# Local attention: scores in quarters of the array, the queries' scale inside the exponentials, a new order of work

## The chip, the cores and the metric

The kernel runs on one core of one Trainium2 chip. The core has TensorE (PE, with PEld for the loading of its stationary operand), VectorE (DVE), ScalarE (ACT), GpSimd (POOL) and SyncE (SP), which only issues transfers here. The metric is the device time of one execution in microseconds (us), lower is better.

## The reference

The input is 16 sequences of 256 tokens with 128 features, so 32 tiles of 128 tokens. The program is: cross attention, a local transformer of depth 2, cross attention again, a mixture of experts. The change is in the attention of the local transformer alone, which is run twice, once for each layer:

```python
h = shift_token(x)
q, k, v = split(h @ wqkv)               # 8 heads of 64
q = q / max(norm(q), 1e-12) * q_scale
k = k / max(norm(k), 1e-12) * k_scale
q, k = rotary_xpos(q, k)                # q * cos + swap_halves(q) * sin, the same for k
# windows of 64 tokens; a query sees its own window and the one before
sim = where(mask, -max, 8 * q @ k.T)    # 64 queries x 128 keys for each head and window
o = softmax(sim) @ v
x = x + o @ wo
```

## The kernel before, in words

Every engine has its own program, written out by hand, and semaphores connect them. The phases stand one behind the other, and all engines meet at the end of each. The phases of local attention (class `Local`, tiles with the prefix `a_`) are the second and the fourth. In such a phase a loop over `s` runs on each engine; in turn `s` the engine does one piece of work for several tiles at once, each at another stage: "`s - 5`" means the tile that came in five turns ago. The order of the pieces within a turn is the order in which the engine does them, and it is this order that the change rewrites. One turn is one tile of 128 tokens.

The stages of one tile, with the lines of the profile:

- L677 to L680, SP: the tile comes into `h`, half of its features shifted by a token. L779, PE: `h` is transposed into `ps_a`. L852, ACT, and L935, DVE, make `hT` and its rounding rest `hTr`.
- L740 to L742, PE: queries and keys into `ps_qk` (two halves of 512 columns, three matmuls each), and with the same lines the values into `ps_b`.
- L872 and L884, ACT: squares of queries and of keys. L921, DVE: their sums for 16 heads (8 of queries, 8 of keys). L997 and L999, POOL: the maximum with 1e-24 and the power -1/2.
- L972 and L975, DVE: products with the table of cosines and, in two pieces of 256 columns with halves swapped, of sines; they go to `rot` and `rot2`. L946, DVE, adds the two for the queries, L995, POOL, for the keys. L1003, POOL, multiplies queries and keys, 1024 columns, by the 16 powers.
- L813, PE: eight transposes of `rot`. L954, DVE: two copies of 64 partitions put the queries into `qbd`, whose other half stays zero, so that the two heads of a pair lie block by block. L878, ACT: the keys into `kTr`.
- L756, PE: the mask is written into the two banks of `ps_s` as a bfloat16 matmul with the identity. L769: eight fp32 matmuls of 128 x 128 add the scores, each for a pair of heads and one window. An fp32 matmul with its weight load has two records each in the trace.
- L928, DVE: maxima over the 128 keys of eight rows. L865, ACT: eight exponentials of 128 x 128 with the maximum as bias, and each followed by the record that reads the accumulated sum. L959, DVE: reciprocals. L1009, POOL: the exponentials, 1024 columns, times the reciprocals.
- L787, PE: eight transposes of the exponentials. L858, ACT: the copy to `eT`, 1024 columns. L803, PE: sixteen matmuls of 64 columns with the values, into two halves of the partitions. L941, DVE: the copy to `oT`. L832, PE: four matmuls with `lwo`. L981, DVE: the sum with the layer's input.
- L891 and L900, ACT: for one window of two tiles the values have to stand in other partitions; half tiles are copied to `vx`. L894 copies the values to `vt`.

The order on ACT in a turn is: L852 (`s - 1`), L858 (`s - 6`), the eight L865 (`s - 5`), L872 (`s - 2`), L878 (`s - 4`), L884 (`s - 2`), L894 (`s - 4`). So tile t's `eT` stands directly ahead of tile t + 1's exponentials. The order on POOL is: L995, L997, L999 and L1003 of tile `s - 3`, then L1009 of tile `s - 5`.

## Time and profile before

| what | us |
|---|---|
| median of 3 runs (1401.6 to 1405.2) | 1403.48 |
| the profiled execution: its own time | 1405.5 |
| its span, first to last instruction | 1403.1 |
| first phase of local attention (from L845 at 228.4 to the last L981 at 539.9), second (629.0 to 945.5) | 311.5, 316.5 |
| busy over the span: PE, DVE, ACT, POOL | 1211.3, 1120.5, 874.9, 877.2 |

The busy times are those of the whole span; the two phases of local attention make up 628 us of it. "Clock" is the TensorE clock that was granted, 1.00 being 2.4 GHz. In the timeline a line stands for one instruction or for several alike in a row ("x8"), with start, length from the first start to the last end, engine and line; a bracket tells for how long the engine had been idle and who released it. Two instructions in a row overlap by a little, so what one costs is the distance between two starts rather than its length.

### The profile page before, as it was taken

Reading aid. Unit: us, or ns where it says so; the run is one execution under the profiler, and the core shown is the slowest. Engines: PE = TensorE matmul, PEld = TensorE weight load, DVE = VectorE, ACT = ScalarE, POOL = GpSimd, SP = SyncE. Lnnn points to the kernel's source line nnn. Section 1 sums busy time; section 2 is a strip of 40 time slices with the busy share of each in tenths; the row PEclk is TensorE's granted clock in tenths of the full one; section 3 lists DMA queues with packets and bytes.
Section 4 is the critical chain, followed back from the end, with each engine's and each line's share of the span. In section 5 each row is a group of like instructions: output and inputs, shape, how many; then the busy total and the mean of one; then the engine's idle time right before and its main releaser. Section 6 shows DMA issues by size and latency. Waiting matters only on the chain.

```text
span 1403.1 us, 32333 instructions
## 1 busy us (share of the span) xinstructions
PE 1211.3 (86%) x10768; PEld 1050.1 (75%) x10768; DVE 1120.5 (80%) x2622; ACT 874.9 (62%) x2445; POOL 877.2 (63%) x1070
## 2 busy tenths in 40 slices
PE   5588774799999994984999999977979999899997
PEld 3466553688888884983788888867966777699997
DVE  3799995899999972775899999946878998488887
ACT  1376662577777772553777777744547777466664
POOL 0567763999999971325999999933346664233342
PEclk9699996999999997996999999998979999899999
DMA  6100000000000001111000000001110000000000
GB/s 166 50 1 2 1 1 15 8 9 9 10 9 9 4 1 47 32 29 23 9 9 9 9 9 8 2 2 30 30 48 2 2 2 1 2 15 13 13 12 14
DMA packets 59411, 23.36 MB, mean 17 GB/s; under 512 B 49093, under 2 KB 57074, under 8 KB 59250
## 3 DMA queue, kind: packets, MB, share of 16 engines
q1 hardware_dynamic: 55296, 19.22, 5.8%
q10 hardware_dynamic: 3954, 2.09, 0.6%
q8 instruction: 90, 1.47, 0.4%
q14 instruction: 71, 0.58, 0.1%
HBM read 10.81 MB, written 2.10 MB: 9 GB/s over the span
## 4 chain that ended last, share of the span: by engine, by line
PE 58%; DVE 18%; issue 9%; ACT 7%; POOL 3%; SPq 2%; DMA 2%; ACTq 1%; DVEq 0%; POOLq 0%
PE a_ps_s L769 7%; PE m_ps_h L1191 7%; PE m_ps_y L1201 6%; DVE x_e L622 5%; DVE x_stat L619 5%; PE a_ps_b L803 4%; PE a_ps_t L813 4%; PE a_ps_t L787 4%; PE f_ps_y L1064 3%; PE a_ps_a L832 3%; PE f_ps_g L1073 3%; PE f_ps_a L1078 3%; ACT a_e L865 3%; ACT x_qhh L531 2%; PE a_ps_s L756 2%
## 5 line engine op out<-in xcount | busy, mean ns | idle before, releaser
L999 POOL TENSOR_TENSOR a_stat<-a_stat,small 128x16 f32<-128x16 f32 x64 | 186.9, 2921 | 5.3
L865 ACT ACTIVATE a_e<-a_ps_s,a_stat 128x128 f32<-128x128 f32 x512 | 179.6, 378 | 4.0 <-DVE a_stat L928 3.1
L769 PEld LDWEIGHTS a_ps_s<-a_kTr,a_qbd 128*128 128x128 f32 x1024 | 137.6, 195 | 4.3
L769 PE MATMUL a_ps_s<-a_kTr,a_qbd 128*128 128x128 f32 x1024 | 137.6, 278 | 0.0
L1009 POOL TENSOR_TENSOR a_e<-a_e,a_stat 128x1024 f32<-128x1024 f32 x64 | 121.4, 1897 | 23.7 <-DVE a_stat L959 23.7
L1003 POOL TENSOR_TENSOR a_rot<-a_rot,a_stat 128x1024 f32<-128x1024 f32 x64 | 121.8, 1903 | 5.0
L865 ACT ACTIVATION_READ_ACCUMULATOR a_e<-a_ps_s,a_stat 128x1 f32 x512 | 111.7, 218 | 0.0
L972 DVE TENSOR_TENSOR a_rot<-a_ps_qk,a_rtab 128x512 f32<-128x512 f32 x128 | 87.9, 687 | 28.3 <-ACT a_sq L872 28.3
L517 ACT ACTIVATE x_e<-x_e 128x1024 f32<-128x1024 f32 x64 | 67.8, 1060 | 68.0 <-DVE x_e L622 68.0
L995 POOL TENSOR_TENSOR a_rot<-a_rot 128x512 f32<-128x512 f32 x64 | 82.5, 1289 | 42.8 <-DVE a_rot L975 42.3
L858 ACT ACTIVATE a_eT<-a_ps_t 128x1024 f32<-128x1024 f32 x64 | 65.5, 1023 | 59.9 <-PE a_ps_t L787 59.9
L1191 PE MATMUL m_ps_h<-m_hT,w 128*128 128x128 f32 x768 | 96.1, 283 | 0.0
L975 DVE TENSOR_TENSOR a_rot<-a_ps_qk,a_rtab 128x256 f32<-128x256 f32 x256 | 95.5, 415 | 0.0
L954 DVE COPY a_qbd<-a_ps_t 64x512 f32<-64x512 f32 x128 | 87.8, 686 | 8.7 <-PE a_ps_t L813 6.7
L1100 ACT ACTIVATE f_gl<-f_ps_g,vec 128x128 f32<-128x128 f32 (+1 forms) x192 | 55.8, 360 | 61.5 <-PE f_ps_g L1073 61.5
L1201 PE MATMUL m_ps_y<-w,m_up 128*128 128x128 f32 x768 | 91.1, 275 | 1.5 <-DVE m_yw L1238 1.5
L1191 PEld LDWEIGHTS m_ps_h<-m_hT,w 128*128 128x128 f32 x768 | 90.9, 196 | 0.0
L482 PE MATMUL x_ps_s<-x_khl,x_qhh 128*128 128x512 f32 x128 | 58.6, 458 | 36.5 <-DVE x_e L622 34.7
L1201 PEld LDWEIGHTS m_ps_y<-w,m_up 128*128 128x128 f32 x768 | 88.3, 192 | 1.6 <-issue 1.6
L928 DVE TENSOR_REDUCE a_stat<-a_ps_s 128x8 f32<-128x1024 f32 x64 | 77.8, 1216 | 11.1 <-PE a_ps_s L769 11.1
L813 PE MATMUL a_ps_t<-c,a_rot 128*128 128x128 f32 x512 | 69.9, 281 | 17.0 <-POOL a_rot L1003 7.5
L1223 ACT ACTIVATE m_up<-m_ps_h 128x512 f32<-128x512 f32 x96 | 57.1, 598 | 43.5 <-PE m_ps_h L1191 43.5
(166 smaller groups left out, 3688.2 us busy)
## 6 DMA issues: line engine op xcount, KB each, us to landing
a_h<-y SPq DMA_DIRECT2D x64, 32.0 KB
f_h<-y SPq DMA_DIRECT2D x64, 32.0 KB
out_dram<-x SPq DMA_DIRECT2D x32, 64.0 KB, 1.5
a_h<-y SPq DMA_DIRECT2D x64, 31.8 KB
f_h<-y SPq DMA_DIRECT2D x64, 31.8 KB
wqkv<-in_L_ffn_wqkv_dram SPq DMA_DIRECT2D x2, 768.0 KB, 4.4
w<-in_L_ffn_w_dram SPq DMA_DIRECT2D x2, 768.0 KB, 5.0
c_ctx2T<-in_ctxT_dram SPq DMA_DIRECT2D x2, 512.0 KB, 3.2
```

Source lines behind the costliest of these rows:

```text
L769: m = pe.matmul(ps_s[:, at:at + P].rearrange("p (w k) -> p w k", k=WIN), self.qbd[u][:, at:at + P], ky, start=False, stop=(c == 3))
L813: m = pe.transpose(ps_t[:, P * i:P * i + P], self.rot[n % 2][:, P * i:P * i + P], g.ident)
L865: act.activation(self.e[n % 2][:, P * i:P * i + P], self.ps_s[:, P * i:P * i + P], ACT.Exp, bias=stat[:, i:i + 1], accum_out=stat[:, 8 + i ...
L954: v.tensor_copy(dst, ps_t[LD * e:LD * e + LD, 0:512].rearrange("p (r q) -> p r q", q=WIN)).then_inc(self.s_qc, 1)
L972: v.tensor_tensor(out1, qk, cos_.unsqueeze(1).broadcast_to([P, LH, LD]), ALU.mult).then_inc(self.s_r, 1)
L975: v.tensor_tensor(out2[:, :, lo:lo + LD // 2], qk[:, :, hi:hi + LD // 2], sin_[:, lo:lo + LD // 2].unsqueeze(1).broadcast_to([P, LH, LD // ...
L995: p.tensor_tensor(r, r, self.rot2[:, INNER:], ALU.add).then_inc(self.s_n, 1)
L999: p.tensor_tensor(t[:, 48:64], t[:, 32:48], g.neg_half.broadcast_to([P, 16]), ALU.pow).then_inc(self.s_n, 1)
L1003: p.tensor_tensor(r, r, t[:, 48:64].unsqueeze(2).broadcast_to([P, 16, LD]), ALU.mult).then_inc(self.s_n, 1)
L1009: p.tensor_tensor(e3, e3, self.stat[n % 2][:, 16:24].unsqueeze(2).broadcast_to([P, 8, P]), ALU.mult)\
L1191: m = pe.matmul(self.ps_h[b][:, P * i:P * i + P], g.w1[:, P * c:P * c + P], self.hT[n % 2][:, :], start=True, stop=True)
L1201: m = pe.matmul(self.ps_y[:, D * e:D * e + D], self.up[n % 2][:, P * c:P * c + P], g.w2[:, D * c:D * c + D], start=(i == 0), stop=(i == w ...
```

## The change

- Scores: `qbd` is gone. One copy of 128 partitions puts the queries' transpose into `qT`. The eight matmuls of 128 x 128 with half of the operand zero become sixteen with 64 rows and 64 columns of the array: head of the pair (`e`) by rows, window (`x`) by columns. The two heads write different banks. The mask's constant is smaller in magnitude and stored once for both windows.
- The power of the queries is no longer multiplied into `rot`. It is given to the exponentials as `scale`, a second pointer operand beside `bias`; the bias is the maximum times that power, a new small product on DVE (`maxima`). POOL multiplies the keys alone, 512 columns.
- The maxima come in two halves of 512 columns, and the exponentials in two groups of four with `kTr` between them.
- The product with the sines is one instruction of 512 columns with reversed halves.
- The copy to `oT` moves from DVE to ACT. ACT's two copies of half tiles to `vx` become transfers on SP's queue.
- The order within a turn is new on PE, ACT, DVE and POOL. On ACT it is: `hT`, `eT`, `vt`, four exponentials, `kTr`, four exponentials, `oT`, two squares. On PE: scores, transpose of `h`, transposes of the exponentials, values, `lwo`, transposes of `rot`, the product with the values, queries and keys. On DVE: rotation of the queries, first maxima, `hTr`, sums of squares, second maxima, `qT`, rotation of the keys, the layer's sum, the queries' addition, reciprocals. On POOL: maximum and power of tile `s - 3`, exponentials times reciprocals of `s - 5`, then addition and product of the keys of `s - 3`. The rotation of a tile is one turn later than before, all other pieces are in the same turn as before.

```diff
-        self.stat = self.many("stat", 2, 64)
-        self.qbd = self.many("qbd", 2, LP * 2 * P)
+        self.stat = self.many("stat", 4, 64)
+        self.qT = self.many("qT", 2, LP * P)
...
-        sp.wait_ge(self.s_z, 4 * l + 2)
-        for n in range(T):
-            k = T * l + n
-            after(sp, self.s_h, k - UNROLL + 1)
-            load_shifted(sp, self.h, self.s_d, self.g.y, n, k)
+        sp.wait_ge(self.s_z, 2 * l + 2)
+        for s in range(T + 5):
+            n = s
+            if 0 <= n < T:
+                k = T * l + n
+                after(sp, self.s_h, k - UNROLL + 1)
+                load_shifted(sp, self.h, self.s_d, self.g.y, n, k)
+            n = s - 5
+            if 0 <= n < T:
+                k, half = T * l + n, slice(0, WIN) if n % 2 else slice(WIN, P)
+                sp.wait_ge(self.s_vc, k + 1)
+                after(sp, self.s_o, k - 3 if n % 2 else k - 2)
+                sp.dma_start(self.vx[n // 2 % 2][half, :], self.vt[n % UNROLL][half, :]).then_inc(self.s_vx[n % 4], 16)
...
+    def scores(self, pe, pair, e, x, u, b):
+
+        rows, at = slice(LD * e, LD * e + LD), P * (LP * e + pair)
+        ky = self.kTr[b % 2][rows, S * pair:S * pair + S].rearrange("p (w k) -> p w k", k=WIN)
+        own, other = local_keys(2 * u + x)
+        if other is None:
+            ky = ky[:, own:own + 1, :].broadcast_to([LD, 2, WIN])
+        elif other < own:
+            ky = ky[:, other:own + 1, :][:, ::-1, :]
+        else:
+            ky = ky[:, own:other + 1, :]
+        dst = self.ps_s[WIN * x:WIN * x + WIN, at:at + P].rearrange("p (w k) -> p w k", k=WIN)
+        return pe.matmul(dst, self.qT[u][rows, P * pair + WIN * x:P * pair + WIN * x + WIN], ky, start=False, stop=(pair == LP - 1))
...
-                pe.wait_ge(self.s_qc, 2 * k + 2)
+                pe.wait_ge(self.s_qc, k + 1)
                 pe.wait_ge(self.s_kc, k + 1)
                 after(pe, self.s_e, 8 * k)
-                for i in range(2):
-                    pe.matmul(ps_s[:, 512 * i:512 * i + 512], g.ident16, g.lmask[:, u, :].unsqueeze(1).broadcast_to([P, 2, 2 * P]),
+                for e in range(2):
+                    pe.matmul(ps_s[:, 512 * e:512 * e + 512], g.ident16, g.lmask[:, u, :].unsqueeze(1).broadcast_to([P, LP, P]),
...
-                        else:
-                            ky = ky[:, own:other + 1, :]
-                        m = pe.matmul(ps_s[:, at:at + P].rearrange("p (w k) -> p w k", k=WIN), self.qbd[u][:, at:at + P], ky,
-                                      start=False, stop=(c == 3))
+                for pair in range(LP):
+                    for e in range(2):
+                        for x in range(2):
+                            m = self.scores(pe, pair, e, x, u, b)
                 m.then_inc(self.s_s, 1)
...
+                after(pe, self.s_vc, k)
+                after(pe, self.s_oc, k - 3)
+                self.project_h(pe, ps_b[:, :], n, 1024).then_inc(self.s_v, 1)
...
+                pe.wait_ge(self.s_nq, k + 1)
+                after(pe, self.s_ec, k - 1)
+                for i in range(2 * LP):
+                    if i == LP:
+                        pe.wait_ge(self.s_n, 4 * k + 4)
+                    m = pe.transpose(ps_t[:, P * i:P * i + P], self.rot[n % 2][:, P * i:P * i + P], g.ident)
+                m.then_inc(self.s_t, 1)
...
+                for i in range(2):
+                    after(pe, self.s_sq, 2 * (k - 1) + i + 1)
+                    after(pe, self.s_r, 4 * (k - 1) + 2 * i + 2)
+                    self.project_h(pe, self.ps_qk[:, 512 * i:512 * i + 512], n, 512 * i).then_inc(self.s_qk, 1)
...
+    def exponentials(self, act, l, n, e):
+
+        if 0 <= n < T:
+            k, stat = T * l + n, self.stat[n % 4]
+            after(act, self.s_et, k - 1)
+            act.wait_ge(self.s_mx, 5 * k + 2 * e + 2)
+            for pair in range(LP):
+                i, h = LP * e + pair, 48 + 2 * pair + e
+                act.activation(self.e[n % 2][:, P * i:P * i + P], self.ps_s[:, P * i:P * i + P], ACT.Exp,
+                               bias=stat[:, 24 + i:25 + i], scale=stat[:, h:h + 1], accum_out=stat[:, 8 + i:9 + i]).then_inc(self.s_e, 1)
 
     def scalar(self, act, l):
...
+            n = s - 4
+            if 0 <= n < T:
+                k, u, b = T * l + n, n % 2, n // 2
+                act.wait_ge(self.s_v, k + 1)
+                after(act, self.s_o, k - 3)
+                after(act, self.s_vx[n % 4], 16 * (k // 4))
+                act.activation(self.vt[n % UNROLL][:, :], ps_b[:, :], ACT.Copy).then_inc(self.s_vc, 1)
+            self.exponentials(act, l, s - 5, 0)
...
+            self.exponentials(act, l, s - 5, 1)
+            n = s - 7
+            if 0 <= n < T:
+                k = T * l + n
+                act.wait_ge(self.s_o, k + 1)
+                after(act, self.s_y, k - 1)
+                act.activation(self.oT[n % 2][:, :], ps_b[:, :], ACT.Copy).then_inc(self.s_oc, 1)
+            n = s - 2
+            if 0 <= n < T:
+                k = T * l + n
+                after(act, self.s_ss, k)
+                act.wait_ge(self.s_qk, 2 * k + 1)
+                act.activation(self.sq[:, 0:INNER], self.ps_qk[:, 0:INNER], ACT.Square).then_inc(self.s_sq, 1)
             n = s - 2
...
+    def maxima(self, v, l, n, e):
+
+        if 0 <= n < T:
+            k, st = T * l + n, self.stat[n % 4]
+            v.wait_ge(self.s_s, k + 1)
+            v.tensor_reduce(st[:, 4 * e:4 * e + 4], self.ps_s[:, 512 * e:512 * e + 512].rearrange("p (r k) -> p r k", k=P), AX_X,
+                            ALU.max, negate=True).then_inc(self.s_mx, 1)
+            v.wait_ge(self.s_mx, 5 * k + 2 * e + 1)
+            v.wait_ge(self.s_n, 4 * k + 2)
+            v.tensor_tensor(st[:, 24 + 4 * e:28 + 4 * e], st[:, 4 * e:4 * e + 4],
+                            st[:, 48:56].rearrange("p (r e) -> p e r", e=2)[:, e, :], ALU.mult).then_inc(self.s_mx, 1)
+
+    def rotate(self, v, l, n, i):
+
+        if 0 <= n < T:
+            k, u, nt = T * l + n, n % 2, UPS * 2 * LD
+            if i:
+                after(v, self.s_n, 4 * (k - 1) + 3)
+            else:
+                after(v, self.s_nq, k)
+            after(v, self.s_t, k - 1)
+            v.wait_ge(self.s_sq, 2 * k + i + 1)
+            at = slice(INNER * i, INNER * i + INNER)
+            qk, out1, out2 = (t[:, at].rearrange("p (h d) -> p h d", d=LD) for t in (self.ps_qk, self.rot[u], self.rot2))
+            lo = 2 * LD * u + LD * i
+            cos_, sin_ = self.rtab[:, lo:lo + LD], self.rtab[:, nt + lo:nt + lo + LD]
+            v.tensor_tensor(out1, qk, cos_.unsqueeze(1).broadcast_to([P, LH, LD]), ALU.mult).then_inc(self.s_r, 1)
+            swapped = qk.rearrange("p h (o d) -> p h o d", o=2)[:, :, ::-1, :]
+            v.tensor_tensor(out2.rearrange("p h (o d) -> p h o d", o=2), swapped,
+                            sin_.rearrange("p (o d) -> p o d", o=2).unsqueeze(1).broadcast_to([P, LH, 2, LD // 2]), ALU.mult)\
+                .then_inc(self.s_r, 1)
...
+            self.rotate(v, l, s - 3, 0)
+            self.maxima(v, l, s - 5, 0)
...
+            self.maxima(v, l, s - 5, 1)
             n = s - 4
             if 0 <= n < T:
                 k = T * l + n
                 v.wait_ge(self.s_t, k + 1)
                 after(v, self.s_s, k - 1)
-                for e in range(2):
-                    dst = self.qbd[n % 2][LD * e:LD * e + LD, :].rearrange("p (r e q) -> p r e q", e=2, q=WIN)[:, :, e, :]
-                    v.tensor_copy(dst, ps_t[LD * e:LD * e + LD, 0:512].rearrange("p (r q) -> p r q", q=WIN)).then_inc(self.s_qc, 1)
+                v.tensor_copy(self.qT[n % 2][:, :], ps_t[:, 0:512]).then_inc(self.s_qc, 1)
+            self.rotate(v, l, s - 3, 1)
+            n = s - 8
+            if 0 <= n < T:
+                v.wait_ge(self.s_y, T * l + n + 1)
+                v.tensor_tensor(tok(g.y2, n), self.ps_a[:, 0:D], tok(g.y, n), ALU.add).then_inc(self.s_yc, 1)
+            n = s - 3
+            if 0 <= n < T:
+                k, r = T * l + n, self.rot[n % 2][:, 0:INNER]
+                v.wait_ge(self.s_r, 4 * k + 2)
...
-        for t in self.qbd:
-            p.memset(t[:, :], 0.0).then_inc(self.s_z, 1)
         for s in range(T + 5):
             n = s - 3
             if 0 <= n < T:
-                k, t = T * l + n, self.stat[n % 2]
+                k, t = T * l + n, self.stat[n % 4]
+                p.wait_ge(self.s_ss, k + 1)
+                after(p, self.s_e, 8 * (k - 3))
+                p.tensor_scalar(t[:, 32:48], t[:, 32:48], 1e-24, None, ALU.max).then_inc(self.s_n, 1)
+                p.wait_ge(self.s_n, 4 * k + 1)
+                p.tensor_tensor(t[:, 48:64], t[:, 32:48], g.neg_half.broadcast_to([P, 16]), ALU.pow).then_inc(self.s_n, 1)
+            n = s - 5
+            if 0 <= n < T:
+                k = T * l + n
+                p.wait_ge(self.s_mx, 5 * k + 5)
+                e3 = self.e[n % 2][:, :].rearrange("p (r k) -> p r k", k=P)
+                p.tensor_tensor(e3, e3, self.stat[n % 4][:, 16:24].unsqueeze(2).broadcast_to([P, 8, P]), ALU.mult)\
+                    .then_inc(self.s_en, 1)
+            n = s - 3
+            if 0 <= n < T:
+                k, t = T * l + n, self.stat[n % 4]
                 r = self.rot[n % 2][:, INNER:]
-                p.wait_ge(self.s_r, 6 * k + 6)
+                p.wait_ge(self.s_r, 4 * k + 4)
                 p.tensor_tensor(r, r, self.rot2[:, INNER:], ALU.add).then_inc(self.s_n, 1)
-                p.wait_ge(self.s_ss, k + 1)
-                p.tensor_scalar(t[:, 32:48], t[:, 32:48], 1e-24, None, ALU.max).then_inc(self.s_n, 1)
-                p.wait_ge(self.s_n, 4 * k + 2)
-                p.tensor_tensor(t[:, 48:64], t[:, 32:48], g.neg_half.broadcast_to([P, 16]), ALU.pow).then_inc(self.s_n, 1)
                 p.wait_ge(self.s_n, 4 * k + 3)
-                p.wait_ge(self.s_nq, k + 1)
-                r = self.rot[n % 2][:, :].rearrange("p (h d) -> p h d", d=LD)
-                p.tensor_tensor(r, r, t[:, 48:64].unsqueeze(2).broadcast_to([P, 16, LD]), ALU.mult).then_inc(self.s_n, 1)
-            n = s - 5
-            if 0 <= n < T:
-                k = T * l + n
-                p.wait_ge(self.s_mx, 2 * k + 2)
-                e3 = self.e[n % 2][:, :].rearrange("p (r k) -> p r k", k=P)
-                p.tensor_tensor(e3, e3, self.stat[n % 2][:, 16:24].unsqueeze(2).broadcast_to([P, 8, P]), ALU.mult)\
-                    .then_inc(self.s_en, 1)
+                r = r.rearrange("p (h d) -> p h d", d=LD)
+                p.tensor_tensor(r, r, t[:, 56:64].unsqueeze(2).broadcast_to([P, LH, LD]), ALU.mult).then_inc(self.s_n, 1)
```

## Rows read from the trace of the kernel before

**Rows 1.** Windows, steady stretch: span, busy time of PE, PEld, DVE, ACT, POOL, clock, DMA.
```profile
300.00:400.00 100.00, 98.04 (x978) 85.97 (x978) 92.49 (x172) 77.23 (x271) 94.35 (x58) 1.00 0.04 10
```

**Rows 2.** Timeline of POOL: the power at both ends of 23.
```profile
300.28 2.92 POOL L999 TENSOR_TENSOR a_stat<-a_stat,small 128x16 f32<-128x16 f32 x1
...
491.94 2.92 POOL L999 TENSOR_TENSOR a_stat<-a_stat,small 128x16 f32<-128x16 f32 x1
```

**Rows 3.** Chain of waits: the transposes of the first tile's exponentials.
```profile
264.89 0.89 PE a_ps_t L787 x8
```

**Rows 4.** Timeline of the last tiles of the first phase: start, length, instruction.
```profile
523.75 0.91 PEld L787 LDWEIGHTS a_ps_t<-c,a_e 128*128 128x128 f32 x8
...
524.93 1.02 ACT L858 ACTIVATE a_eT<-a_ps_t 128x1024 f32<-128x1024 f32 x1 [1.81 <-PE a_ps_t L787]
...
525.98 0.37 ACT L865 ACTIVATE a_e<-a_ps_s,a_stat 128x128 f32<-128x128 f32 x1
...
528.64 0.24 ACT L865 ACTIVATION_READ_ACCUMULATOR a_e<-a_ps_s,a_stat 128x1 f32 x1
...
529.20 1.90 POOL L1009 TENSOR_TENSOR a_e<-a_e,a_stat 128x1024 f32<-128x1024 f32 x1 [5.92 <-DVE a_stat L959]
531.14 1.56 PEld L787 LDWEIGHTS a_ps_t<-c,a_e 128*128 128x128 f32 x8 [4.27 <-POOL a_e L1009]
```

**Rows 5.** Chain of waits in the steady stretch: start, length, instruction.
```profile
377.43 0.89 PE a_ps_t L787 x8
378.32 1.08 PE a_ps_b L803 x32
...
379.52 1.06 PE a_ps_t L813 x8
...
381.98 0.89 PE a_ps_a L832 x8
382.87 0.23 PE a_ps_b L740
...
383.57 0.23 PE a_ps_s L756
383.80 0.89 PE a_ps_s L769 x8
...
385.80 0.24 PE a_ps_a L779
```

**Rows 6.** Timeline of POOL as the pipeline fills.
```profile
259.22 1.90 POOL L1003 TENSOR_TENSOR a_rot<-a_rot,a_stat 128x1024 f32<-128x1024 f32 x1
261.07 1.90 POOL L1009 TENSOR_TENSOR a_e<-a_e,a_stat 128x1024 f32<-128x1024 f32 x1
```

**Rows 7.** Timeline of DVE in the steady stretch.
```profile
379.45 0.69 DVE L941 COPY a_oT<-a_ps_b 128x512 f32<-128x512 f32 x1
380.05 0.68 DVE L946 TENSOR_TENSOR a_rot<-a_rot 128x512 f32<-128x512 f32 x1
...
385.32 0.28 DVE L981 TENSOR_TENSOR y<-a_ps_a,y 128x128 f32<-128x128 f32 x1
```

**Rows 8.** Timeline of ACT: two instructions of 128x512 in a row.
```profile
382.02 0.63 ACT L872 ACTIVATE a_sq<-a_ps_qk 128x512 f32<-128x512 f32 x1
382.50 0.65 ACT L878 ACTIVATE a_kTr<-a_ps_t 128x512 f32<-128x512 f32 x1
```

**Rows 9.** Timeline of ACT in the dense layer and in the experts' phase.
```profile
603.20 0.87 ACT L1100 ACTIVATE f_gl<-f_ps_g,vec 128x128 f32<-128x128 f32 x3 [0.88 <-PE f_ps_g L1073]
...
1336.46 0.28 ACT L1213 ACTIVATE m_hT<-m_ps_x 128x128 f32<-128x128 f32 x1 [0.64 <-PE m_ps_x L1181]
1336.64 0.17 ACT L1219 ACTIVATE m_rt<-m_ps_r 128x8 f32<-128x8 f32 x1
```

**Rows 10.** ACT by groups: count, busy time, mean ns of one.
```profile
L1100 ACT ACTIVATE f_gl<-f_ps_g,vec 128x128 f32<-128x128 f32 x128 | 39.9, 363 | 61.5 <-PE f_ps_g L1073 61.5
...
L1092 ACT ACTIVATE f_hT<-f_ps_x,vec 128x128 f32<-128x128 f32 x64 | 29.3, 457 | 37.3 <-PE f_ps_x L1056 36.9
```

More of the change, by code:

```diff
@@ L35 @@
 AWAY = -2.0e38
+LOCAL_AWAY = -1.0e24
 PADDED = -1.0e38
@@ L699, in __init__ @@
         self.s_d = first.s_d if first else [g.sem(f"a_d{i}") for i in range(UNROLL)]
-        self.s_vx = first.s_vx if first else [g.sem(f"a_vx{i}") for i in range(2)]
+        self.s_vx = first.s_vx if first else [g.sem(f"a_vx{i}") for i in range(4)]
     def begin(self, l):
@@ new lines, in tensor @@
+                m.then_inc(self.s_t, 1)
+            n = s - 7
+            if 0 <= n < T:
+                k, u, b = T * l + n, n % 2, n // 2
+                pe.wait_ge(self.s_ec, k + 1)
+                if u:
+                    pe.wait_ge(self.s_vx[n % 4 - 1], 16 * (k // 4 + 1))
+                    pe.wait_ge(self.s_vx[n % 4], 16 * (k // 4 + 1))
+                after(pe, self.s_oc, k)
+                pe.wait_ge(self.s_vc, min(k + 4, T * l + T))
+                for pair in range(LP):
+                    for x in range(2):
+                        vv = self.vx[b % 2] if 2 * u + x == 2 else self.vt[n % UNROLL]
+                        for e in range(2):
+                            at = P * (LP * e + pair) + WIN * x
+                            m = pe.matmul(ps_b[LD * e:LD * e + LD, P * pair + WIN * x:P * pair + WIN * x + WIN],
+                                          vv[:, P * pair + LD * e:P * pair + LD * e + LD],
+                                          self.eT[u][:, at:at + WIN], start=True, stop=True)
+                m.then_inc(self.s_o, 1)
@@ L845, in scalar @@
         act.activation(self.wqh[:, :], g.wqkv[:, :], ACT.Copy).then_inc(self.s_wh, 1)
-        for s in range(T + 6):
+        for s in range(T + 7):
             n = s - 1
@@ L895, in scalar @@
-            n = s - 5
-            if 0 <= n < T and n % 2 == 0:
-                k, b = T * l + n, n // 2
-                act.wait_ge(self.s_vc, k + 1)
-                after(act, self.s_o, k - 2)
-                act.activation(self.vx[b % 2][WIN:P, :], self.vt[n % UNROLL][WIN:P, :], ACT.Copy).then_inc(self.s_vx[0], 1)
+    def maxima(self, v, l, n, e):
[8 more added lines that the diff above has]
+                            st[:, 48:56].rearrange("p (r e) -> p e r", e=2)[:, e, :], ALU.mult).then_inc(self.s_mx, 1)
```

155 lines of the change are left out of this document (29 added, 126 removed).

## The prediction

> **What bounds the kernel now.** I read four views. The windows first: in a steady stretch of local attention PE is busy 98.0 of 100 us, POOL 94.4, DVE 92.5, ACT 77.2 [rows 1]. So three engines are close to full, and taking work from one of them alone can give little. Then the period: 23 powers on POOL, one per tile, start from 300.28 to 491.94 us [rows 2], which is 22 turns of 8.71 us. Over a whole phase the transposes of the exponentials (L787, which I call C) go from 264.89 for tile 0 [rows 3] to 531.14 for tile 31 [rows 4]: 266.25 us for 31 turns, 8.59 each. Third, the chain of waits: in the steady stretch it is PE from end to end, and one turn reads off it as C 0.89, product with values 1.08, transposes of `rot` 1.06, six matmuls for queries and keys of 0.23, `lwo` 0.89, values 0.70 (382.87 to 383.57), twice a mask of 0.23 and scores of 0.89, and 0.24 for the transpose of `h` [rows 5]. That makes 8.5, and some tenths of "issue" between. Read alone this says: PE is the bound, shorten its scores and the turn shortens. The fourth view is why I don't stop there: at the phase's end, where PE has little left to do, the timeline shows a loop that no engine's busy time shows [rows 4].
>
> **The loop through the softmax.** In it C of tile 30 begins at 523.75 us, ACT copies to `eT` at 524.93, the exponentials of tile 31 begin at 525.98 and their last sum is read by 528.88, the reciprocal follows, POOL multiplies from 529.20 to 531.10, and C of tile 31 begins at 531.14. That is 7.39 us from C to C with no engine in the way. It is a real loop: ACT does `eT` of tile t ahead of the exponentials of tile t + 1, `eT` needs C, C needs POOL's product, and this needs all eight sums of its own tile. Before, 7.39 fits below 8.71. The question for the change is what it puts into this loop.
>
> **The change part by part, engine sums.** PE: the scores are 2 x 0.89 for eight matmuls [rows 5]. The new sixteen have 32 records like the product with the values, where two halves of columns work at once and 32 records take 1.08 [rows 5]. All four quarters at once would need no more than that: 3.56 us one after another (sixteen, each as long as one of the four in 0.89), divided by four is 0.89. I take 1.08. PE falls from 8.71 to about 8.0. If only columns overlap and rows don't, it is 3.56 / 2 = 1.78, no gain. No row of before shows two row groups at work; these are the two bounds, and I take 1.08 since the column halves do overlap. POOL: busy 8.2 a turn, minus half of a 1.90 product [rows 6], about 7.3. DVE: 8.05 busy, minus the copy to `oT` (0.60 from start to start [rows 7]), minus one of two `qbd` copies (the same 0.60), plus a second start of the maxima and two products of four columns, estimated at 0.2 each and nothing else, about 7.3. The one product with swapped halves stands between 0.60 (its size [rows 7]) and what its two halves took; this changes nothing below. ACT: 6.7 busy, `oT` in for `vx`, both some 0.48 per tile [rows 8]. The transfers for `vx` have two turns, 16 us, between the values and their first reader; the loads on SP ahead of them are asked for two turns early too, so both are hidden. If that cover were gone, PE would wait on them, and nothing else would. The memsets of `qbd` go; they lay beside the first transfers and are worth nothing. By these sums no engine would be above 8.0, and the turn would fall by 0.7.
>
> **What enters the loop.** Three things.
> (1) `vt` now stands between `eT` and the exponentials: 0.48 us, the distance between two starts of 128x512 on ACT [rows 8]. Its input is ready in time: values follow C on PE, 0.89 + 0.70 us after C's start, and `eT` begins 1.18 and ends 2.2 after it.
> (2) `kTr` stands between the two groups of four: another 0.48.
> (3) Each of eight exponentials has a second pointer operand. The trace of before has the price. A 128x128 activation without pointers takes 0.28 us (L1213 [rows 9]), with one 0.363 (L1100), with two 0.457 (L1092 [rows 10]), so the second costs 0.094. And it isn't hidden when they come in a row: three with one pointer take 0.87, (0.87 - 0.36) / 2 = 0.255 from start to start, while the one without has its follower after 0.18 [rows 9]. That is 0.075. I take 0.085 between the two, 8 x 0.085 = 0.68. Nothing in before has an exponential with both pointers and a sum read behind each, so the bounds are 0 (the reading hides it) and 0.094.
> The loop becomes 7.39 + 0.96 + 0.68 = 9.03 us. That is longer than 8.71 and longer than any engine's sum. Nothing is taken out of it: the halved maxima, the queries' product and the scores all lie outside.
>
> A rule of the Trainium skill speaks against this edit: "ScalarE: Activation LUTs", section "What ACT_TABLE_LOAD costs", has it that each pointer operand of an activation adds about 93 ns and that activations in a row overlap by about 93 ns whatever they carry. The rows agree on the length (0.094). By its figure the eight would cost 0.74 and the turn would be 9.1.
>
> **Do the others keep up at 9.03?** From C's start the exponentials end after 5.13 + 0.96 + 0.68 = 6.77. DVE's reciprocal stands last in its turn, behind `qT`, which waits for the transposes of `rot`: C 0.89, values 0.70, `lwo` 0.89, transposes 1.06 and 0.04 to the release [rows 5] is 3.58; then four of 0.60 (`qT`, two products, the addition [rows 7]) and 0.28 for the layer's sum make 6.26 or so. It is ready before the sums are. As a loop of its own (on to C by 0.28 + 1.90 + 0.04 [rows 4]) it has 8.5 us: this is what would hold if the exponentials were fast. PE, from the end of the exponentials: about 0.1 to the release, masks 0.46, scores 1.08, two changes of the array's shape of about 0.2 (the "issue" pieces), `h` 0.24 is 2.3, just what the path over POOL takes (531.14 - 528.88 = 2.26). So with all four quarters at work PE is not late. With 1.78 for the scores it is 0.5 to 0.7 late, and the turn is 9.6 or 9.7.
>
> **Fill and end of a phase.** POOL now does the product of exponentials and reciprocals ahead of the keys' product (in before tile 0's waited behind 1.86 us of L1003 [rows 6]), and for each of the first tiles it has some 0.9 less to do. Tile 0 should reach C about 4 us sooner (an estimate; bounds 0 and 6). The last turn has neither `vt` nor `kTr`. One phase: 30 x 9.03 + (7.39 + 0.68) = 279.0 against 266.25, so 12.7 more, 4 back, 8.7 us longer. Two phases are 17.4. On the profiled execution's 1405.5 that gives 1422.9; it lay 2.0 above the median, so I say 1421 us.
>
> **Rivals.**
> *A, the pointer is hidden* behind the reading of the sum that follows each exponential, which takes 0.24 [rows 4]. For it: no row has this pair. Against it: the other pointers show in the distance of starts. The softmax loop would be 8.35, DVE's loop of 8.5 would hold, and a phase would be 30 x 8.5 + 7.4 - 4 - 266.25 = 7.9 us shorter: 1388 us. This is the one on the other side, and it decides at a turn of 8.75 (31 turns with a short last one equal 266.25 + 4), which is 0.05 per exponential.
> *B, row groups don't overlap.* Scores take 1.78, PE is the late one and a turn has 9.6 or so: 30 x 0.57 us more in each phase, some 1455. For it: the trace shows only halves of columns at once. Against it: nothing in the rows. The Trainium skill, "TensorEngine Tiling (Array Packing)", key properties, says that different tiles of the array load and multiply in parallel and that a change of the tiling mode drains the engine; by it B falls away, while two drains a turn come in, which the 0.2 above already stand for.
> *C, the busy shares are right* and the loop gives way: the turn is PE's 8.0, 1403.5 - 2 x (31 x 0.6 + 3), some 1360. It needs `eT` or the exponentials not to wait as I read them, and [rows 4] has that wait in it.
> *D, the parts cancel*: a pointer of 0.04 to 0.05, or more given back in the fill: 1399 to 1408.
>
> **How the numbers follow.** The forecast, a turn of 8.85 to 9.3, holds 1411 to 1437 with the fill's bounds, chance 0.50. B has 0.10, A 0.18, C 0.06, D 0.16, of which 0.11 lie within 0.3% of 1403.5 (4.2 us, about what a measurement tells here), 0.04 above and 0.01 below. Faster is A + C + 0.01 = 0.25, same 0.11, slower 0.64. The range goes from A with its own spread, 1382, to 1448, between the forecast and B: it leaves out C, most of B and the ends of the forecast.
>
> **What would show it.** Steps of POOL's power at 9.0. ACT idle about 2 us ahead of `eT` with PE's transposes as releaser, POOL idle ahead of the product with the reciprocals, released by DVE's reciprocal, and PE idle ahead of C, released by POOL. Exponentials about 0.43 from start to start instead of 0.34. Scores of about 1 us for 32 records. The chain of waits would go ACT, DVE, POOL, PE instead of PE alone. If the exponentials stay at 0.34, A holds; if PE is never idle and the scores take 1.8, B; a C that begins before POOL's product of the same tile has ended would break the whole reading.

## The result and the profile after

| | us |
|---|---|
| before, median (4 runs, 1401.6 to 1405.95) | 1404.34 |
| after, median (4 runs, 1422.51 to 1425.8) | 1424.6 |
| ratio, 95% interval | 1.0137, 1.012 to 1.0154 |
| after: the profiled execution, its span | 1424.4, 1422.6 |
| busy over the span: PE, DVE, ACT, POOL | 1198.0, 1072.6, 913.4, 819.2 |

The change makes the kernel 1.4% slower. I look first at the same windows as in [rows 1] (columns: span, busy time of PE, PEld, DVE, ACT, POOL, granted clock, DMA):

```profile
300.00:400.00 100.00, 93.74 (x1126) 70.24 (x1126) 81.81 (x158) 81.79 (x261) 82.36 (x58) 1.00 0.11 24
```

No engine is full any more. PE was at 98.0 and is at 93.7, POOL fell by 12 and DVE by 11 points, and yet a turn takes longer. The power on POOL, one per tile, at both ends of 23 (22 turns):

```profile
301.09 2.91 POOL L1014 TENSOR_TENSOR a_stat<-a_stat,small 128x16 f32<-128x16 f32 x1
...
497.26 2.91 POOL L1014 TENSOR_TENSOR a_stat<-a_stat,small 128x16 f32<-128x16 f32 x1
```

196.17 / 22 is 8.917 us a turn, against 8.71 [rows 2]. The chain of waits, 369 to 400 us, has as its summary and as one turn:

```profile
by line: ACT a_e L864 35.1%; POOL a_e L1020 24.6%; issue 22.5%; PE a_ps_t L799 14.3%; ACT a_kTr L897 4.7%; DVE a_stat L1000 2.1%; ACT a_vt L890 1.1%; ACT a_eT L883 0.6%; ACTq L861 0.2%
...
376.44 1.91 POOL a_e L1020
378.39 1.11 PE a_ps_t L799 x8
379.56 0.66 issue
...
380.44 0.09 ACT a_vt L890
...
380.92 1.09 ACT a_e L864 x5
...
382.79 0.49 ACT a_kTr L897
...
384.01 1.04 ACT a_e L864 x4
385.07 0.21 DVE a_stat L1000
...
385.35 1.91 POOL a_e L1020
387.31 1.11 PE a_ps_t L799 x8
```

In [rows 5] every piece was PE's. Now the chain is the softmax loop of [rows 4], turn after turn: C (now L799) at 378.39, `eT` 379.52, `vt` 380.44, first exponential 380.92, `kTr` among them, reciprocal 385.07, POOL 385.35, C at 387.31, 8.92 later. The waits of 300 to 400 us say the same from the side of the engines (total, times, longest):

```profile
ACT a_eT L883 <- PE a_ps_t L799: 12.6, 12, 1.1
POOL a_e L1020 <- DVE a_stat L1000: 12.1, 11, 1.1
...
PEld a_ps_t L799 <- POOL a_e L1020: 4.7, 11, 0.4
```

And the timeline of ACT shows the price of the second pointer operand:

```profile
380.92 0.46 ACT L864 ACTIVATE a_e<-a_ps_s,a_stat 128x128 f32<-128x128 f32 x1
381.26 0.21 ACT L864 ACTIVATION_READ_ACCUMULATOR a_e<-a_ps_s,a_stat 128x1 f32 x1
381.35 0.47 ACT L864 ACTIVATE a_e<-a_ps_s,a_stat 128x128 f32<-128x128 f32 x1
```

0.43 from start to start, where the kernel before has 0.344 (x4, which is before with its exponentials untouched, starts them at 377.65 and 377.99 in a steady turn).

### The profile page after: what moved, and what is told of

The parts are those of the page before. It is cut to its first block, busy times and chain, and to the rows that moved or that the text cites. A ratio compares the mean times of both kernels' runs of the same rounds, so it can differ in the third digit from the quotient of the medians.

```text
span 1422.6 us, 34602 instructions
## 1 busy us (share of the span) xinstructions
PE 1198.0 (84%) x11792; PEld 972.8 (68%) x11792; DVE 1072.6 (75%) x2558; ACT 913.4 (64%) x2445; POOL 819.2 (58%) x1066
## 4 chain that ended last, share of the span: by engine, by line
PE 29%; ACT 21%; DVE 19%; issue 16%; POOL 10%; DMA 2%; SPq 2%; ACTq 1%; DVEq 0%; POOLq 0%
ACT a_e L864 14%; POOL a_e L1020 8%; PE m_ps_h L1211 6%; PE m_ps_y L1221 6%; DVE x_e L621 5%; DVE x_stat L618 5%; PE a_ps_t L799 5%; ACT a_kTr L897 2%; PE f_ps_y L1084 2%; PE f_ps_g L1093 2%; ACT x_qhh L530 2%; PE f_ps_a L1098 2%; DMA f_h<-y 1%; ACT x_hT L522 1%; DVE y L259 1%
## 5 line engine op out<-in xcount | busy, mean ns | idle before, releaser
L864 ACT ACTIVATE a_e<-a_ps_s,a_stat 128x128 f32<-128x128 f32 x512 | 229.9, 483 | 0.0
L944 DVE TENSOR_TENSOR a_rot<-a_ps_qk,a_rtab 128x512 f32<-128x512 f32 x128 | 87.8, 686 | 51.9 <-ACT a_sq L911 50.6
L864 ACT ACTIVATION_READ_ACCUMULATOR a_e<-a_ps_s,a_stat 128x1 f32 x512 | 118.3, 231 | 0.0
L923 DVE TENSOR_REDUCE a_stat<-a_ps_s 128x4 f32<-128x512 f32 x128 | 86.8, 678 | 13.0 <-PE a_ps_s L763 13.0
L799 PE MATMUL a_ps_t<-c,a_e 128*128 128x128 f32 x512 | 74.3, 291 | 24.8 <-POOL a_e L1020 24.8
L946 DVE TENSOR_TENSOR a_rot<-a_ps_qk,a_rtab 128x512 f32<-128x512 f32 x128 | 87.0, 680 | 0.0
L799 PEld LDWEIGHTS a_ps_t<-c,a_e 128*128 128x128 f32 x512 | 59.3, 148 | 36.9 <-POOL a_e L1020 36.9
L551 ACT ACTIVATE x_eT<-x_ps_t 128x1024 f32<-128x1024 f32 x64 | 65.4, 1022 | 24.5 <-PE x_ps_t L496 24.5
L747 PE MATMUL a_ps_qk<-a_wqh,a_hT 128*128 128x512 f32 x128 | 64.1, 501 | 19.1 <-DVE a_rot L946 13.4
L621 DVE TENSOR_TENSOR x_e<-x_ps_s,x_stat 128x1024 f32<-128x1024 f32 x64 | 78.4, 1224 | 2.2
```

The lines of the kernel that those rows point to most:

```text
L621: v.tensor_tensor(self.e[n % 2][:, :].rearrange("p (h k) -> p h k", k=SC), sc, self.stat[n % 2][:, 0:XH].unsqueeze(2).broadcast_to([P, XH, ...
L799: m = pe.transpose(ps_t[:, P * i:P * i + P], self.e[n % 2][:, P * i:P * i + P], g.ident)
L864: act.activation(self.e[n % 2][:, P * i:P * i + P], self.ps_s[:, P * i:P * i + P], ACT.Exp, bias=stat[:, 24 + i:25 + i], scale=stat[:, h:h ...
L923: v.tensor_reduce(st[:, 4 * e:4 * e + 4], self.ps_s[:, 512 * e:512 * e + 512].rearrange("p (r k) -> p r k", k=P), AX_X, ALU.max, negate=Tr ...
L944: v.tensor_tensor(out1, qk, cos_.unsqueeze(1).broadcast_to([P, LH, LD]), ALU.mult).then_inc(self.s_r, 1)
L946: v.tensor_tensor(out2.rearrange("p h (o d) -> p h o d", o=2), swapped, sin_.rearrange("p (o d) -> p o d", o=2).unsqueeze(1).broadcast_to( ...
```

## The experiments

"Turn" is the distance of two powers on POOL in the steady stretch of the first phase. Ratios are to the kernel before, timed on the same chip beside each run (its median there lay between 1403.5 and 1404.7). x1 and x7 leave the queries' scaling out of the result; all others compute the whole.

| run | median us | ratio, 95% interval | turn us |
|---|---|---|---|
| before | 1404.3 | | 8.71 |
| after | 1424.6 | 1.0137 (1.012 to 1.0154) | 8.917 |
| x1 constant scale | 1385.02 | 0.9858 (0.9841 to 0.9874) | 8.408 |
| x2 copy inside the loop | 1459.02 | 1.0384 (1.0367 to 1.0402) | 9.43 |
| x3 copy outside it | 1439.35 | 1.025 (1.0233 to 1.0267) | 8.45 and 9.99 by turns |
| x4 before, quarters only | 1402.73 | 0.9987 (0.9978 to 0.9997) | 8.70 |
| x5 row groups apart | 1433.66 | 1.0197 (1.0164 to 1.0231) | 8.95 |
| x6 halves | 1414.96 | 1.0081 (1.0066 to 1.0096) | 8.28 and 9.41 by turns |
| x7 halves, constant scale | 1377.61 | 0.9804 (0.9781 to 0.9827) | 8.28 |
| x8 halves, C split | 1394.86 | 0.9936 (0.9915 to 0.9956) | 8.465 |
| x9 x8, rest of `h` earlier | 1414.48 | 1.0066 (1.0054 to 1.0078) | 8.86 |
| x10 x3, rest of `h` earlier | 1428.32 | 1.0169 (1.0154 to 1.0184) | 8.99 |
| x12 before, pointer only | 1448.93 | 1.032 (1.0304 to 1.0337) | 9.44 |
| x13 x9, small product later | 1403.62 | 0.9995 (0.9981 to 1.0009) | 8.68 |

**x1, from after.** Is it the pointer?

```diff
-  bias=stat[:, 24 + i:25 + i], scale=stat[:, h:h + 1], accum_out=...
+  bias=stat[:, 24 + i:25 + i], scale=1.0, accum_out=...
```

> The changed kernel, but the exponentials' scale is the constant 1.0 instead of the pointer to the queries' power (so the queries' scores are not scaled; the bias is still the product). My theory (the pointer costs time inside the softmax loop): an exponential goes from 0.434 us start to start to 0.34, the softmax loop of 8.92 us falls to 8.2, and DVE's loop (queries' transposes, rotation of the keys, addition, reciprocal, POOL, transposes: 8.4 in the trace of the changed kernel) takes over: a turn of 8.4, 62 turns by 0.5, about 1394 us. Rival (the added copies in the loop are the whole matter, the pointer is hidden): 1420 to 1425. Rival (POOL or PE bound): no change.

39.6 us less than after, and faster than before. The powers:

```profile
298.79 2.91 POOL L1014 TENSOR_TENSOR a_stat<-a_stat,small 128x16 f32<-128x16 f32 x1
...
492.18 2.92 POOL L1014 TENSOR_TENSOR a_stat<-a_stat,small 128x16 f32<-128x16 f32 x1
```

193.39 / 23 = 8.408. The exponentials are at 0.34 again (382.54, 382.88, 383.22), so the softmax loop would be 0.72 shorter, 8.20, and what holds is DVE's loop, which the prediction put at 8.5: the chain of waits goes POOL, C, values, `lwo`, transposes of `rot`, `qT`, rotation of the keys, the layer's sum, addition, reciprocal, POOL, and names no instruction of ACT. 62 turns of 0.51 less are 31.6 of the 39.6; where the rest lies I didn't trace. The pointer decides the sign.

**x2 and x3, from after.** One copy more of 128x512 on ACT, once inside and once outside the softmax loop.

```diff
+  act.activation(self.spare[:, :], g.c32[:, 0:INNER], ACT.Copy).then_inc(self.s_sp, 1)
   # x2: ahead of exponentials(act, l, s - 5, 0); x3: behind the copy to oT
```

> The changed kernel with one more copy of 128x512 on ACT per turn, from a constant to a spare tile, between the values' copy and the first group of exponentials. Theory (the loop sets the turn): the whole length of the copy is paid, 0.5 us a turn, 31 x 2 turns, about 1424.6 + 31 = 1455. Rival (some engine's sum or PE's order sets the turn; ACT has 1.6 us of idle time per turn): less than 5 us more.

> The same spare copy, but behind the copy to oT, ahead of the squares, so after the exponentials of the turn. Theory: it eats idle time of ACT (1.05 us ahead of eT, 0.6 ahead of hT) and of DVE (0.87 us ahead of the rotation): within 3 us of the changed kernel, 1424.6. Rival (ACT's amount of work sets the turn): 1455 as in the other place.

Inside it cost 34.4 us, the 0.51 a turn that its 0.48 should. Outside it should have been free, and cost 14.7: turns of 8.45 and 9.99 alternate. The waits of x3, 300 to 400 us, that after doesn't have or has shorter:

```profile
DVE a_rot L949 <- ACT a_sq L916: 14.1, 11, 1.4
...
PE a_ps_a L817 <- DVE a_hTr L976: 5.2, 6, 0.9
```

Every other turn `lwo` waits for DVE's rest of `h`. The copy makes the square of the queries late, and with it everything on DVE behind it. So close below the softmax loop of after there is a second one, which I hadn't seen: exponentials, `oT`, squares on ACT; rotation of the queries, maxima, rest of `h` on DVE; `lwo` and transposes of `rot` on PE; `qT`, rotation of the keys, addition and reciprocal on DVE; POOL; C. In the long turns, and only there, one thing more stands in it, the small product of the first four maxima. It begins just behind the start of POOL's product of the keys and ends with it:

```profile
390.70 1.04 POOL L1035 TENSOR_TENSOR a_rot<-a_rot,a_stat 128x512 f32<-128x512 f32 x1
390.72 1.04 DVE L932 TENSOR_TENSOR a_stat<-a_stat 128x4 f32<-128x4 f32 x1
```

In the short turn before, it began ahead of POOL's (381.61 against 381.79) and took 0.17. The 0.87 more are as long as the wait of `lwo`, so the hold has a part in the second loop's length. **x10** tests the loop: the copy of x3, and the rest of `h` ahead of the first maxima.

```diff
   self.rotate(v, l, s - 3, 0)
-  self.maxima(v, l, s - 5, 0)
   ...  # hTr of tile s - 1
+  self.maxima(v, l, s - 5, 0)
```

> The copy outside the softmax loop again (128x512 on ACT, behind oT and ahead of the squares), but with DVE's rest of h ahead of the first maxima. The copy alone cost 14.7 us, which I had not expected. If the cost came by a second loop (late square, rotation of the queries, maxima, rest of h, lwo, transposes of rot, qT), taking 0.7 to 1.0 us of maxima out of that chain leaves it below 8.92: the turn is 8.92 again and the time 1424 to 1428. Rival: the chain doesn't go through the rest of h, and the time stays at 1439 within 0.3%.

11 of the 14.7 us are gone and that wait with them: the second loop it was, and it went through the rest of `h`. The turn is 8.99, not 8.92. The small product is still held in every turn (0.92 at 388.51), and now the sum of squares, `qT` and the rotation of the keys come late behind it, for which PE waits:

```profile
PE a_ps_qk L749 <- DVE a_rot L951: 7.3, 11, 0.7
```

No run takes the hold alone out of x3, so how the 14.7 divide between the loop's own length and the hold isn't shown.

**x4, from before: the scores in quarters and nothing else.** (`scores`, `qT` and the mask as in the change's diff; the rest of before stands.)

> The kernel before with one part of the change alone: scores in quarters of the array, with the single copy to qT, the mask and the indices that go with it. Everything else (order, POOL's product of queries and keys, exponentials with one pointer, copies to vx and oT) as before. What the chain of waits of before says alone (PE is the bound, 0.75 us less of scores per turn): a turn of 8.0, about 1404 - 45 = 1360. My theory: PE was not alone at 8.7; DVE from the rotation to the maxima (5.1), the exponentials (2.8), the square and the releases (0.8) make a loop of 8.6, so a turn of 8.5 to 8.65 and 1392 to 1400 us. If quarters did not overlap at all: 1404 or more.

```profile
300.00:400.00 100.00, 90.12 (x1145) 72.58 (x1147) 83.83 (x161) 77.26 (x269) 94.35 (x58) 1.00 0.04 9
```

A miss by every theory, and the one that says most about the kernel before. PE has 8 points less to do than in [rows 1], and the turn is 8.70. The quarters alone are worth 0.1%. The chain (summary, 369 to 400 us) and a wait:

```profile
by line: ACT a_e L869 34.6%; DVE a_rot L974 17.7%; issue 14.4%; DVE a_stat L932 7.9%; ACT a_sq L876 7.3%; DVE a_rot L977 7.0%; DVE a_stat L925 5.3%; PE a_ps_t L791 2.9%; DVE y L983 2.7%; PE a_ps_a L783 1.0%; DVEq L969 0.6%; ACT a_eT L862 0.
```
```profile
PE a_ps_a L783 <- DVE y L983: 8.5, 11, 0.8
```

It is a loop of exponentials, square, DVE's two rotations and its addition to `y`, then either PE's transposes of `h` and C with `eT` behind them or DVE's sum and maxima, then exponentials again. It takes as long as PE's whole turn did. So before wasn't bound by PE alone: a loop through the exponentials was as long.

**x12, from before: the pointer and nothing else**, which must tell the two readings of before apart.

```diff
-  bias=stat[:, i:i + 1], accum_out=...
+  bias=stat[:, i:i + 1], scale=g.one, accum_out=...
```

> The kernel before, with a pointer to a column of ones as scale of its exponentials: the second pointer operand alone, same result. By the prediction's reading of the kernel before (PE alone bounds the turn of 8.71, the softmax loop has 7.39) the eight times 0.09 make that loop 8.1 and cost nothing: 1403 to 1406. By what the kernel before with only the scores in quarters showed (the turn stays at 8.70 with PE at 90%), a second loop through the exponentials, the square, DVE's rotations, the sum of squares and the maxima was as long as PE's: then 0.09 x 8 = 0.72 comes on top of 8.7, and the time is up to 62 x 0.7 higher, about 1447.

44.3 us slower than before, with a turn of (493.79 - 304.93) / 20 = 9.44, which is 0.73 more:

```profile
304.93 2.92 POOL L999 TENSOR_TENSOR a_stat<-a_stat,small 128x16 f32<-128x16 f32 x1
...
493.79 2.92 POOL L999 TENSOR_TENSOR a_stat<-a_stat,small 128x16 f32<-128x16 f32 x1
```

The eight pointers are on the path in full in the kernel before too. The place is seen in the timelines of ACT and PE:

```profile
375.25 0.62 ACT L872 ACTIVATE a_sq<-a_ps_qk 128x512 f32<-128x512 f32 x1
375.73 0.63 ACT L878 ACTIVATE a_kTr<-a_ps_t 128x512 f32<-128x512 f32 x1
```
```profile
376.45 0.38 PE L756 MATMUL a_ps_s<-c 128*128 128x512 bf16 x1 [0.42 <-issue]
```

The mask waits for `kTr`, which ACT does behind exponentials and square. Masks and scores, `h` and C follow on PE, then `eT` and the exponentials. That loop has 9.44 here, and 0.72 less, 8.72, without the pointer. The chain of waits of x12, even so, names PE from end to end with "issue" for the gap (7.3%).

**x5, from after: the row groups one behind the other.** All even heads' matmuls, then all odd ones.

```diff
-  for pair in range(LP):
-      for e in range(2):
+  for e in range(2):
+      for pair in range(LP):
```

> The sixteen score matmuls are issued in another order: all of the even heads first, then all of the odd ones, so that neighbours in the stream share their 64 rows of the array and differ only in the half of columns. If the four quarters of the array work side by side only when neighbours in the stream lie in different ones, the scores go from 1.04 us to about 1.78 (half of the 3.56 that sixteen matmuls take one after another). In the kernel after, the transpose of h that follows the scores ends 0.24 us before POOL's product lets C begin, so the turn grows by 0.74 - 0.24 = 0.5 us to about 9.4, and the time by 62 x 0.5 to about 1455: this is rival B of the prediction, made on purpose. Rival: the order of issue is of no account, because the array takes any matmul whose quarter is free: scores stay at 1.04 and the time at 1424.6 within 0.3%.

```profile
381.37 1.59 PE L763 MATMUL a_ps_s<-a_kTr,a_qT 64*64 64x128 f32 x32
382.89 0.33 PE L791 MATMUL a_ps_a<-c,a_h 128*128 128x128 f32 x1
383.06 1.04 PE L799 MATMUL a_ps_t<-c,a_e 128*128 128x128 f32 x8
```

The scores take 1.52 instead of 1.03: the order of issue does count, but costs 0.49 and not the 0.74 expected. The steady turn is 8.95, only 0.03 more, so PE had some 0.45 of room ahead of C and not the 0.24 that I read off one wait. The chains of waits have the other 0.2: C takes 1.11 in after, where its weight load waits up to 0.4 for POOL, and 0.89 in x5, where the load waits for nothing. The rest of the 9 us isn't in the steady turn. The traced execution, the slowest of four that go from 1427.3 to 1439.6, has it in the first turns of a phase, and there the granted clock differs (third, fourth and fifth turn):

| | us | granted clock |
|---|---|---|
| before, first phase | 8.36, 10.06, 8.42 | 0.80, 1.00, 1.00 |
| before, second phase | 8.40, 10.06, 8.42 | 0.82, 0.98, 1.00 |
| after, first phase | 9.21, 9.01, 8.92 | 0.81, 1.00, 1.00 |
| after, second phase | 10.64, 9.42, 10.09 | 0.68, 0.82, 1.00 |
| x5, first phase | 10.33, 10.99, 10.41 | 0.67, 0.75, 0.94 |
| x5, second phase | 11.01, 10.99, 10.38 | 0.69, 0.75, 0.94 |

After itself loses 3.0 us so in its second phase. Whether the order of the scores brings the lower clock about or met it by chance, no run tells, so the 9 us aren't the price of the order; 0.03 a turn is.

**x6, x7, x8, from after: shorten the softmax loop.** Reciprocal and POOL's product in two halves, the first as soon as four exponentials are done. x7 has the constant scale in addition, x8 lets PE begin C with the first half.

```diff
+  self.recip(v, l, s - 5, 0)          # behind the keys' rotation; recip(.., 1) at the end
...
+  for e in range(2):                  # POOL: 512 columns each
+      p.wait_ge(self.s_mx, 6 * k + 5 + e)
...
+  if i == LP: pe.wait_ge(self.s_en, 2 * k + 2)      # x8, in front of the fifth transpose
```

> The reciprocal and POOL's product are done in two halves: the first four heads' once the first four exponentials are summed, while the other four are still under way. Only the second half then stands in the softmax loop: one product of 512 instead of 1024 columns, about 1.05 us (what POOL's product of the keys takes) instead of 1.90. My theory: the loop falls from 8.92 to about 8.07 us, DVE's loop from 8.4 to 7.8, PE's sum is 8.0, so the turn is 8.1 (8.05 to 8.3) and the time 1424.6 - 62 x 0.82, about 1374, faster than the kernel before by 2%. Rival: the second loop that the copy outside the softmax loop brought to light (squares, rotation of the queries, maxima, rest of h, lwo, transposes of rot) lies at 8.4 to 8.9 by itself and takes over: 1392 or more.

> The halves of the run before, and the exponentials with a constant scale of 1.0 instead of the pointer (this leaves the queries' scaling out of the result). My theory: with halves the softmax loop stands at about 8.07, only just above PE's sum, so taking out the 8 x 0.09 of the pointer brings the loop to 7.4 but the turn only to PE's 8.0: 1365 to 1374, at most 0.6% less than with halves alone. Rival: the pointer's 0.09 comes off in full, as it did from the kernel after (39.6 us): about 1335.

> The halves, and the transposes of the exponentials on PE begin as soon as the first half of the product is done; the last four wait for the second. In the softmax loop this takes out another 0.5 us (four of the eight transposes): about 7.6. My theory: PE's sum of 8.0 then holds, the turn is 8.0 to 8.1 and the time 1366 to 1374, within 0.5% of the halves alone. Rival: PE waits in the middle of the transposes for the second half, so its own work behind them isn't moved forward, and the time is that of the halves alone or up to 5 us more.

x6 misses by 41 us: turns of 8.28 and 9.41 alternate, as in x3. x8 misses too, by 21, but gets 1394.9, 0.6% faster than before and the fastest that keeps the whole computation. x7 comes out at 1377.6, 4 us above its range: PE is full there by its busy time (98.86 of 100), so 8.28 is what this order of PE's work takes, with a wait of 0.18 for POOL in it (C's weight load, which delays C as in after). The long turns of x6 have what those of x3 have, in the timelines of DVE and POOL:

```profile
386.38 0.94 DVE L927 TENSOR_TENSOR a_stat<-a_stat 128x4 f32<-128x4 f32 x1
```
```profile
386.26 1.04 POOL L1035 TENSOR_TENSOR a_rot<-a_rot,a_stat 128x512 f32<-128x512 f32 x1
```

A product of four columns takes 0.94, and ends where POOL's ends (387.32 and 387.30). In the short turns it takes 0.51, held by the end of POOL's addition; unheld, in x8, it has 0.16.

**x9 and x13.** x9 is x8 with the rest of `h` ahead, as in x10. x13 puts, in addition, that small product behind the sum of squares.

```diff
   self.maxima(v, l, s - 5, 0)         # x13: the reduction alone
   ...  # reduce_sum of the squares
+  self.rooted(v, l, s - 5, 0)         # x13: the product of four columns
```

> The halves with the split transposes, and on DVE the rest of the transposed h (hTr, 0.2 us) moved ahead of the first maxima, so that lwo on PE no longer waits for it. With halves and split alone the turn was 8.46 us and lwo took 1.06 to 1.07 from its forerunner to its follower where its eight matmuls need 0.89; the same kernel with a constant scale had 8.29, all of it PE. My theory: the turn falls to 8.3 and the time by 62 x 0.16, to about 1385. Rival: the maxima come 0.2 later, the exponentials with them, and nothing is won: 1392 to 1396.

> As the run with halves, split and the earlier rest of h (1414.5 us, a miss: turn 8.86), but DVE's small product of the first four maxima (128x4, both inputs in SBUF) stands behind the sum of squares instead of ahead of it. In that run this product began at 379.77 us, 0.02 after POOL had begun its product of the keys (379.75, 1.04 us), and took 1.04 instead of 0.17: it ended with POOL's. My theory: the two engines exclude each other while both have two operands in SBUF, and the 0.87 went into the chain maxima, sum, second maxima, qT, rotation of the keys, projections on PE. Behind the sum (1.1 us later) POOL's product is over: the product takes 0.17 again, the turn falls by 0.5 to 8.3 or 8.4 and the time to 1383 to 1392, faster than the kernel before. Rival: the place of the rest of h itself made that run slow, and the time stays above 1408.

x9 loses 20 us to x8, where 10 were to be won. DVE's product came 0.02 us behind POOL's start, where in x8 it had come 0.06 ahead of it (381.62 and 381.68):

```profile
379.77 1.04 DVE L929 TENSOR_TENSOR a_stat<-a_stat 128x4 f32<-128x4 f32 x1
```
```profile
379.75 1.04 POOL L1037 TENSOR_TENSOR a_rot<-a_rot,a_stat 128x512 f32<-128x512 f32 x1
```

In x13 it takes 0.15 again and the turn falls, but to 8.68 and not to 8.3, and the time to 1403.6, which is that of before: the exponentials now wait for it behind the sum of squares (product at 380.02, first exponential at 380.27), and exponentials, `oT`, square, rotation, maxima and sum are a loop of 8.68. So the stretched product was real and could be taken away, but my figure for the turn behind it was wrong: the first exponentials pay for the new place.

## Why the prediction was right

1421 was forecast, 1424.6 came, for the reason given. By its own steps:

- **Softmax loop of 9.03: measured 8.917, and it is the chain.** `vt` 0.48 (380.44 to 380.92) and `kTr` 0.49, as said. The pointer is 0.090 an exponential (0.434 against 0.344), 8 x 0.09 = 0.72 against 0.68. No run takes `vt` or `kTr` out of the loop again; x2 shows that a copy in their place is paid in full. The base was too long: of the 1.05 from `eT` to the exponentials [rows 4] only 0.92 is the copy (379.52 to 380.44). The rest belongs to the end of the phase: in a steady turn of before it is 0.92 too (378.35 to 379.27).
- **Rival A, price 1388, DVE's loop 8.5.** x1 gives 1385.0 and 8.41. The pointer isn't hidden, but what would be without it was priced rightly.
- **Rival B** falls: 32 records of the scores take 1.03 with four quarters at work. I had taken 1.08.
- **PE's sum of 8.0** was a little too low. x7 shows 8.28 with PE full, of which some 0.2 is C's wait for POOL (C 1.08; behind the same scores it has 0.87 in x8, where its load doesn't wait). That leaves 8.1. In the chain of x7 the first matmul behind the product with the values, where the array's shape changes, takes 0.43 instead of 0.23, and the one that opens the second half 0.47, where it doesn't change. I counted the changes of shape in PE's path to C and forgot them in its sum.
- **PE "just as late" as POOL at C:** it is not, by 0.45 (x5): a wait of 0.24, and 0.2 by which C itself gets shorter when PE comes late.
- **Fill, 4 us sooner:** 2.2 (C of tile 0 at 262.5 against 264.7). At the end of phase one after is 7.8 us behind (C of tile 31 at 538.9 and 531.1), predicted 8.7; at the end of phase two 18.8 (955.4 and 936.7), predicted 17.4. That the total comes so near is in part luck: the turn was 0.11 shorter than forecast, the fill gave back less, and phase two cost 11.0 and not 7.8 again, of which 3.0 are its third to fifth turn at the lower clock (table at x5). The prediction had no term for the clock.
- **Signs:** ACT is idle for 1.05 us ahead of `eT`, not for 2; the other waits that were named are there.
- **What the prediction had wrong without paying for it** is its reading of before. It said that PE alone makes the turn of 8.71 and that a loop of 7.39 lies well below. x4 and x12 show loops through the exponentials of 8.7. The 7.39 were right to 0.13 for the loop that was read, but the others hadn't been walked. By the prediction's reading the pointer alone would have cost before nothing; it cost 44.3 us. With the quarters' 1.7 gained, that would be 1447. After has 1424.6, so the new order of work gives back some 22 us, if the parts add up, which no run shows.

By the Trainium skill, "ScalarE: Activation LUTs", "What ACT_TABLE_LOAD costs", the pointer would be 93 ns. The 0.09 between two starts agrees, with a read of the sum behind each too.

## What to carry to other kernels

A full engine in the chain of waits doesn't say that it alone sets the turn. Walk each loop that crosses engines and add up its instructions in the steady stretch, ahead of trusting the busy shares: here PE's own order and two loops through the exponentials stood at 8.7, and relieving PE alone bought 0.1%. A small price per instruction (0.09) counts by how often it stands in such a loop: on eight exponentials a turn it was worth 40 us. What helped was to cut the loop: half a reciprocal and product early, and C split (0.6% faster than before). And look at the length of each small instruction in the loop, turn by turn: one of 0.16 us that another engine holds for 0.9 is not seen in any sum.

## What the runs showed of the hardware

- **A DVE product with two SBUF inputs waits for POOL's product or addition to end.** A 128x4 product of 0.16 us is stretched to 0.43 in after, to 0.92 in x10, to 0.94 in x6 and to 1.04 in x3 and x9, each time to the end of the POOL instruction that began before it. In after, where it stands outside the chain:

```profile
379.15 0.43 DVE L927 TENSOR_TENSOR a_stat<-a_stat 128x4 f32<-128x4 f32 x1
```
```profile
378.29 1.28 POOL L1027 TENSOR_TENSOR a_rot<-a_rot 128x512 f32<-128x512 f32 x1
```

  Both end at about 379.57. DVE instructions with another number or place of inputs run beside POOL at their usual length: the maxima (378.43, 0.68) beside this addition, the sum of squares (379.71, 1.20) beside the product of the keys (379.64, 1.04). It isn't all of POOL's work: at 381.54, during the power (381.33, 2.92 us), the same product takes 0.16. The Trainium skill, "SBUF — State Buffer", "SBUF: two separate sides", has the pair of ports as an exclusive lock for the whole instruction, taken by a DVE instruction with two SBUF inputs against a POOL instruction that reads SBUF. The held products agree. The power has SBUF inputs too and doesn't hold the product up; why, no run here shows.
- **Four quarters of the array work side by side:** 32 records of 64x64 in 1.03 us, where one after another they would take 3.56 by the prediction's estimate. In an order where neighbours share their rows it is 1.52, between that and the 1.78 of my estimate.
- **Turns can alternate** (8.28 and 9.41 in x6, 8.45 and 9.99 in x3). In both the small product is held for longer in the long turns (0.94 against 0.51, 1.04 against 0.17); that it begins ahead of POOL's product in one turn and behind it in the next goes with the alternation, and what starts it isn't shown. A mean over turns hides this; the single starts show it.
- **The first turns of a phase run partly at the lower clock** (1.2 GHz), and not equally in each: after's third turn has a mean of 0.81 in the first phase and 0.68 in the second, behind a turn at 0.99 and 1.00 in which PE was busy for 6.2 of 7.8 us and for 6.0 of 7.6.
